# Causal attention: transposing the probabilities of query rows 4 to 7 by VectorE and transfers instead of TensorE

## What is computed

```python
qkv = jnp.einsum('bse,ehd->bshd', x, qkv_w) + qkv_b
q, k, v = jnp.split(qkv, 3, axis=-1)
logits = jnp.einsum('bqhd,bkhd->bhqk', q, k)
logits = logits / jnp.sqrt(jnp.asarray(q.shape[-1], logits.dtype))
mask = jnp.tril(jnp.ones((q.shape[1], q.shape[1]), dtype=jnp.bool_))
logits = jnp.where(mask, logits, _large_negative_number(logits.dtype))
probs = jax.nn.softmax(logits, axis=-1)
attn = jnp.einsum('bhqk,bkhd->bqhd', probs, v)
return jnp.einsum('bqhd,hde->bqe', attn, out_w) + out_b
```

## Time and profile before

| | before |
|---|---|
| runs | 1651.46, 1652.03, 1653.18 us |
| median | 1652.03 us |
| profiled execution: span | 1651.1 us |
| TensorE busy | 1635.6 us (99%), 9922 matmuls |
| VectorE busy | 1330.1 us (81%) |
| ScalarE busy | 1005.6 us (61%) |
| GpSimd busy | 888.1 us (54%) |
| granted TensorE clock, mean | 0.999 |

### The profile page before, as it was taken

How to read it: one execution, slowest core, us unless ns; L and a number is a source line. 1 busy time by engine, 2 the same in 40 slices (tenths; PEclk the granted TensorE clock), 3 DMA queues, 4 the chain that set the end, 5 groups by cost and what they waited for, 6 DMA issues and landing times.

```text
span 1651.1 us, 29212 instructions
## 1 busy us (share of the span) xinstructions
PE 1635.6 (99%) x9922; PEld 1044.6 (63%) x9922; DVE 1330.1 (81%) x2763; ACT 1005.6 (61%) x2025; POOL 888.1 (54%) x686
## 2 busy tenths in 40 slices
PE   8999999999999999999999999999999999999998
PEld 6765566556655665566556655665666766676767
DVE  7677777777777778777777777776999999999997
ACT  4466666666666666666666666666676557566562
POOL 4133333334333333433333433334999999999995
PEclk9999999999999999999999999999999999999999
DMA  8000000000000000000000000010000000000000
GB/s 182 27 1 1 2 1 1 1 2 1 1 1 1 1 1 1 1 1 2 1 1 1 1 2 1 1 27 1 1 1 7 7 1 8 7 2 7 1 7 13
DMA packets 30036, 13.55 MB, mean 8 GB/s; under 512 B 17066, under 2 KB 29380, under 8 KB 29892
## 3 DMA queue, kind: packets, MB, share of 16 engines
q1 hardware_dynamic: 29892, 11.70, 3.1%
HBM read 9.60 MB, written 2.10 MB: 7 GB/s over the span
## 4 chain that ended last, share of the span: by engine, by line
PE 96%; DVE 2%; ACT 1%; issue 1%; POOL 0%; DVEq 0%; POOLq 0%; ACTq 0%
PE pair L1007 17%; PE flip L1024 17%; PE accum L1045 11%; PE pair L2755 9%; PE misc L972 7%; PE flip L2778 5%; PE misc L1091 4%; PE flip L2767 4%; PE misc L985 3%; PE accum L1069 3%; PE flip L2815 3%; PE accum L2767 2%; PE accum L2778 2%; PE accum L1073 2%; PE flip L2801 1%; PE flip L949 1%
## 5 line engine op out<-in xcount | busy, mean ns | idle before, releaser
L391 POOL TENSOR_SCALAR probs<-probs,recip 128x256 f32<-128x256 f32 (+5 forms) x448 | 331.2, 754 | 688.2 <-DVE recip L647 688.0
L466 ACT ACTIVATE probs<-pair,neg_max 128x768 f32<-128x768 f32 (+5 forms) x448 | 332.0, 749 | 208.9 <-DVE neg_max L629 208.9
L629 DVE TENSOR_REDUCE neg_max<-pair 128x1 f32<-128x768 f32 (+7 forms) x512 | 372.3, 753 | 32.8 <-PE pair L1007 9.6
L1024 PEld LDWEIGHTS flip<-ident,probs 128*128 128x128 f32 x2048 | 228.0, 141 | 142.3 <-issue 65.4
L1007 PE MATMUL pair<-qk_sb 64*128 64x512 f32 (+3 forms) x1536 | 291.6, 505 | 0.8 <-ACT probs L466 0.7
L1024 PE MATMUL flip<-ident,probs 128*128 128x128 f32 x2048 | 280.0, 277 | 1.8 <-ACT slots L428 1.8
L428 ACT ACTIVATE slots<-flip 128x512 f32<-128x512 f32 x320 | 183.6, 595 | 155.7 <-PE flip L1024 155.7
L620 DVE TENSOR_TENSOR pair<-pair,mask 128x128 f32<-128x128 f32 x512 | 136.9, 292 | 79.4 <-PE pair L1007 79.4
L1045 PE MATMUL accum<-slots,v_sb 128*64 128x512 f32 (+3 forms) x1024 | 192.7, 519 | 0.0
L2755 PE MATMUL pair<-slow_sb,h_T 128*128 128x512 f32 x384 | 179.9, 594 | 1.2 <-ACT probs_last L466 1.0
L1587 POOL TENSOR_TENSOR prod<-xnT,qs 128x1024 f32<-128x1024 f32 (+3 forms) x32 | 180.2, 5639 | 0.9 <-DVE qs L2296 0.9
(11 more groups left out here) (230 smaller groups left out, 2542.0 us busy)
## 6 DMA issues: line engine op xcount, KB each, us to landing
out<-x SPq DMA_DIRECT2D x8, 256.0 KB, 2.3
x<-in_L_attn_x SPq DMA_DIRECT2D x3, 512.0 KB, 5.8
slow_sb<-in_L_attn_w_slow SPq DMA_DIRECT2D x3, 512.0 KB, 8.0
w_qk<-in_L_attn_qkv_w SPq DMA_DIRECT2D x2, 512.0 KB, 7.5
xn<-in_L_ffn_W SPq DMA_DIRECT2D x1, 1024.0 KB
x<-in_L_attn_x SPq DMA_DIRECT2D x2, 256.0 KB, 3.3
w_v<-in_L_attn_qkv_w SPq DMA_DIRECT2D x1, 512.0 KB, 8.1
bv_bc<-in_L_attn_qkv_b SPq DMA_DIRECT2D x1, 512.0 KB, 8.0
```

Of the source, the lines that this page charges most:

```text
L391: pool.tensor_scalar(part, part, recip[:, u % 2, row, h:h + 1], 0.0, ALU.mult, ALU.add).then_inc(scaled, 1)
L466: act.activation(dst, pair[h][:, lo:hi], ACT.Exp, bias=neg_max[:, u % 2, row, h:h + 1], accum_out=row_sum[:, u % 2, row, h:h + 1]).then_in ...
L629: dve.tensor_reduce(out=neg_max[:, u % 2, row, h:h + 1], in_=pair[h][:, lo:hi], axis=AX.X, op=ALU.max, negate=True).then_inc(max_ready, 1)
L1024: last = pe.transpose(flips[bank][:, P * k:P * (k + 1)], src[:, P * k:P * (k + 1)], ident[:])
```

## The change

The probabilities of query rows 4 to 7 are no longer transposed by TensorE. ScalarE writes them to a new buffer `big` with the 128 keys of each block cut into four groups of 32, so that for a key group `b` all its blocks of both heads lie together. GpSimd scales them there. VectorE transposes them in place, every 32x32 block for itself (`turn`, eight instructions a unit, one for each row and head). What is left is to exchange blocks between groups of 32 partitions: SyncE issues for each row sixteen SBUF-to-SBUF transfers (`move`), one from each of four source groups of partitions to each of four target groups, 32 partitions by 256 (r + 1) bytes, from `big` to `across`. That is 64 transfers a unit. `weigh_high` reads `across` in runs of 32 columns, in two groups: rows 6 and 7, then rows 4 and 5.

With it go these changes:
- Rows 0 to 3 are still flipped by TensorE, only their own 10 blocks a head (`flip`, names f0 to f3), kept by ScalarE alone in `low_T`; `weigh_low` reads them.
- Row 3 no longer uses `pair`. Its scores go to the two flip banks (`score_last`), so that `pair` holds four steps a unit.
- The three banks flip 0, flip 1 and `misc` are one pool (`BANK`, `take`).
- The mask is added once for a step, to all its rows and both heads (`cover`).
- The bias of the values is added to the attention (`keep_att`) instead of the values; ScalarE now keeps values, projections and the attention.
- Everything of a unit's transposing and weighing is done one unit later, and all orders are new.

The diff, cut to its core:

```diff
+HIGH_ROWS = (6, 7), (4, 5)
+DEEP = 8, 6
+LOW = 4
...
-LAST_BANK = 0
...
+BANK = {('f1',): 0, ('f0',): 2, ('f2', 1): 1, ('v', 1): 2, ('v', 0): 2, ('f3', 1): 0, ('f2', 0): 1, ('qk', 1, 0): 2, ('f3', 0): 0, ('qk', 1, 1): 2, ('qk', 0, 1): 2, ('o', 0): 0, ('qk', 0, 0): 2, ('o', 1): 1}
+MOVES = P // 32
...
+        big = sb("big", [P, MOVES * 64 * sum(r + 1 for g in HIGH_ROWS for r in g)])
+        across_flat = sb("across", [P, MOVES * 2 * 64 * sum(DEEP)])
+        low_T = sb("low_T", [P, 2, LOW, 512])
...
-        probs = sb("probs", [P, 2, 2, S])
...
-        slots = sb("slots", [P, (2 * ROWS + 1) * 512])
...
+        probs_low = e_buf[:].rearrange("p c n -> p (c n)"), qs[:].rearrange("p c n -> p (c n)")
...
+        def probs_of(row, h):
+
+            if row < LOW:
+                return probs_low[h][:, LOW_AT[row]:LOW_AT[row] + P * (row + 1)]
+            return row_probs[row][:, :, :, 32 * h:32 * (h + 1)]
...
+            def move(u, row):
+                if done(u):
+                    return
+                g = group_of(row)
+                sp.wait_ge(turned[row], 2 * (u + 1))
+                if u:
+                    sp.wait_ge(weighed, weighed_at(u - 1, "high", g))
+                else:
+                    sp.wait_ge(branch_ready, 2 * B)
+                i = HIGH_ROWS[g].index(row)
+                for a in range(MOVES):
+                    for b in range(MOVES):
+                        sp.dma_start(across[g][32 * b:32 * (b + 1), a, i, 0:row + 1, :], row_probs[row][32 * a:32 * (a + 1), b, :, :]
+                                     ).then_inc(moved[row], 16)
+
+            for u in range(UNITS):
+                move(u - 1, 6)
+                move(u - 1, 5)
+                move(u - 1, 4)
+                move(u, 7)
+            tails["sync"] = move
 
...
-                part = probs_last[:, h, :] if step_of(row) == LAST else probs[:, h, step_of(row) % 2, lo:hi]
+                part = probs_of(row, h)
...
+                if row >= LOW:
+                    if u:
+                        act.wait_ge(moved[row], 16 * MOVES * MOVES * u)
+                    dst = dst.rearrange("p b j k -> p j b k")
+                    src = src.rearrange("p (j b k) -> p j b k", b=MOVES, k=32)
...
+                wide = mask[:].unsqueeze(1)
+                if len(STEP_ROWS[step]) == 2:
+                    wide = wide.unsqueeze(1).broadcast_to([P, 2, 2, P])
+                else:
+                    wide = wide.broadcast_to([P, 2, P])
+                dve.tensor_tensor(part, part, wide, ALU.add).then_inc(covered, 1)
...
+            def turn(u, row, h):
...
+                part = probs_of(row, h)
+                dve.wait_ge(scaled, scaled_at(u, row, h))
+                dve.transpose(part, part).then_inc(turned[row], 1)
...
+            def score_last(u):
...
+                for h in range(2):
...
+                    part = slice(D * h, D * (h + 1))
+                    pe.matmul(flips[h], lhsT=q[part, P * r:P * (r + 1)], rhs=k[part, 0:512], start=True, stop=True
+                              ).then_inc(bank_made[h], 1)
...
+            def flip(u, name, *h):
...
+                k = take(u, name, *h)
+                row = int(name[1])
+                for n, each in enumerate(h if h else range(2)):
+                    pe.wait_ge(scaled, scaled_at(u, row, each))
+                    for c in range(row + 1):
+                        at = P * ((row + 1) * n + c)
+                        last = pe.transpose(pool_of[k][:, at:at + P], probs_of(row, each)[:, P * c:P * (c + 1)], ident[:])
+                last.then_inc(bank_made[k], 1)
...
-            def weigh_high(u, lo, hi):
...
+            def weigh_high(u, g, lo, hi):
...
+                    for row in HIGH_ROWS[g]:
+                        pe.wait_ge(moved[row], 16 * MOVES * MOVES * (u + 1))
...
+                for j in range(lo, hi):
+                    own = int(j == DEEP[g] - 1)
+                    for h in range(2):
+                        dst = accum[D * h:D * (h + 1), 0:2 * P].rearrange("p (a i q) -> p a i q", a=MOVES, i=2)[:, :, own:2, :]
+                        last = pe.matmul(dst, lhsT=values_of(u, j, h), rhs=across[g][:, :, own:2, j, 32 * h:32 * (h + 1)],
+                                         start=j == 0, stop=j == DEEP[g] - 1)
+                if hi == DEEP[g]:
+                    weighed_at.meet(u, "high", g)
+                    last.then_inc(weighed, 1)
...
+                for j in range(LOW):
...
+                        last = pe.matmul(accum[D * h:D * (h + 1), P * j:512], lhsT=values_of(u, j, h), rhs=low_T[:, h, j, P * j:512],
+                                         start=j == 0, stop=j == LOW - 1)
...
+            last_move = tails["sync"]
+            last_move(UNITS - 1, 6)
+            last_move(UNITS - 1, 5)
+            last_move(UNITS - 1, 4)
```

More of the change, by code:

```diff
@@ L109, in banks_of, with __init__ @@
     return [k for k in range(2) if lo < 512 * (k + 1) and hi > 512 * k]
-GROUPS = (1, 0)
-EARLY = (('qk', 0, 1), ('qk', 1, 0))
+GROUPS = (0, 1)
+EARLY = (('qk', 1, 0), ('qk', 1, 1))
 class Tally:
-    def __init__(self, order, last=()):
+    def __init__(self, order, last=(), tail=()):
         self.order, self.at, n = order, {}, 0
         for body in range(-1, UNITS + 1):
-            for key, ahead in order:
+            for key, ahead in [(key, -1) for key in tail] if tail and body == UNITS else order:
                 if 0 <= body + ahead < UNITS or (body + ahead == UNITS and key in last):
@@ L462, in softmax @@
-                if owner >= 0:
-                    for f in range(1 if before == LAST else 2):
-                        bank = FLIP_BANK[before, h, f]
-                        act.wait_ge(flipped[bank], flips_at[bank](owner, before, h, f))
-                act.activation(dst, pair[h][:, lo:hi], ACT.Exp, bias=neg_max[:, u % 2, row, h:h + 1],
-                               accum_out=row_sum[:, u % 2, row, h:h + 1]).then_inc(probs_ready, 1)
-            def keep_att(u, g):
+                if step_of(row) != LAST:
+                    exps_at.meet(u, row, h)
@@ L614, in cover @@
-            def cover(u, row, h):
-                if done(u):
-                    return
-                covers_at.meet(u, row, h)
-                lo, hi = place_of(row)
-                dve.wait_ge(scores_ready, scores_at(u, step_of(row), banks_of(row)[-1]))
-                dve.tensor_tensor(pair[h][:, hi - P:hi], pair[h][:, hi - P:hi], mask[:], ALU.add).then_inc(covered, 1)
+                covers_at.meet(u, step)
+                part = diagonals(step)
+                if step == LAST:
+                    for h in range(2):
+                        dve.wait_ge(bank_made[h], uses_at[h](u, "s4"))
+                else:
+                    dve.wait_ge(scores_ready, max(scores_at(u, step, k) for k in range(2)))
@@ L992, in score @@
                 scores_at.meet(u, step, bank)
-                if step == 0:
-                    pe.wait_ge(misc_kept, max(misc_at(u, "qk", c, half) for c in range(2) for half in range(2)))
-                before, owner = (step - 1, u) if step else (LAST, u - 1)
-                if before == LAST and bank != LAST_BANK:
-                    before = LAST - 1
+                projected(u)
+                before, owner = (step - 1, u) if step else (LAST - 1, u - 1)
                 if owner >= 0:
-                    pe.wait_ge(probs_ready, max(exps_at(owner, r, h) for r in STEP_ROWS[before] if bank in banks_of(r) for h in range(2)))
+                    for r in STEP_ROWS[before]:
+                        if bank in banks_of(r):
+                            for h in range(2):
+                                pe.wait_ge(*exponents_of(owner, r, h))
                 q, k = qk_sb[:, u % 2, 0, :], qk_sb[:, u % 2, 1, :]
@@ L1018, in flip, with free_accum @@
+            def free_accum(u, *part):
+                use = weighed_at(u, *part)
                 if use > 1:
-                    pe.wait_ge(flip_kept[bank], use - 1)
+                    pe.wait_ge(att_kept, use - 1)
                 else:
-                    pe.wait_ge(ffn_added, 2 * (B - 1))
-                src = probs_last[:, h, :] if step == LAST else probs[:, h, step % 2, 512 * f:512 * (f + 1)]
-                for k in range(GB):
-                    last = pe.transpose(flips[bank][:, P * k:P * (k + 1)], src[:, P * k:P * (k + 1)], ident[:])
@@ L1025, in flip, with has_values @@
-                last.then_inc(flipped[bank], 1)
-            def weigh_high(u, lo, hi):
+                    pe.wait_ge(ffn_added, 2 * B)
+            def has_values(u, f):
+                for i in range(2):
+                    k, use = use_of(u - u % 2 + f, "v", i)
+                    pe.wait_ge(bank_kept[k], use)
+            def weigh_high(u, g, lo, hi):
                 if done(u):
@@ L1052, in weigh_first, with weigh_low @@
+                if hi == DEEP[g]:
+                    weighed_at.meet(u, "high", g)
+                    last.then_inc(weighed, 1)
+            def weigh_low(u):
```

(3 more changed lines are left out.)

797 lines of the change are left out of this document (393 added, 404 removed).

## The result

The changed kernel takes 1968.19 us (median of 4 runs, 1965.68 to 1971.22) against 1652.59 us (1651.46 to 1653.18): **1.191 times as long, 95% interval 1.189 to 1.193**. The forecast was 1516, with a range from 1468 to 1600 and a chance of 0.08 for the mechanism that came.

A forecast was written before the change was run, and what follows sets the result against it. TensorE, full at 33.06 us a unit, was taken as the bound; afterwards the softmax loop at 28.4. Saving 149.1 over 32 units, less 1.7 and 11.7, turned a 1651.1 span into 1515.4; forecast 1516 us, range 1468 to 1600.

The forecast's parts named there:

- The SyncE queue: SyncE issuing 64 transfers a unit at 0.41 us each: 26.3 us, just under TensorE's 26.8; bounds 0.31 to 0.55.
- a step of the queue above 0.45: Sign, in SyncE's transfers of a row, that the forecast is wrong in size; starts 0.41 us apart were expected.
- slower by the same mechanism: Rival: at 0.51 us a transfer SyncE's queue cancels the whole gain; at 0.55 the time is 1732; chance 0.08.
- The end: After unit 31, next layer's first transposes wait for row 4's transfers: 25.9 us instead of 14.2, losing 11.7.
- VectorE: VectorE's load falls from 24.65 to 23.4 us a unit, with eight new block transposes costing 8.2.
- The rival that pays per block: VectorE's transposes pay 0.292 us for each 128-column block, 15.2 us a unit; time 1615 to 1665; chance 0.08.
- ScalarE, GpSimd: Loads a unit: ScalarE 20.1 us after copies go and come, GpSimd 12.1 us with its scaling unchanged.
- The ring: Four score steps a unit, each waiting for earlier exponentials to read its bank: 7.0, 6.9, 7.2, 7.3, sum 28.4 us.
- the steps of rows 6 and 0 and of rows 4 and 2: Two of the four score steps a unit, summed through masks, maxima and exponentials: 6.9 and 7.3 us.
- TensorE's floor: TensorE's own work a unit: 33.06 less 6.3 us for 52 transposes gone, 26.8 us.
- the weighing in runs of 32 columns: TensorE's matmuls over high rows reading columns in runs of 32 elements: priced at nothing extra; weighing 5.90 us before.
- the four projections: TensorE's projections in a unit, priced from start to start at 0.86 us each.

The follow-up runs named there:

- p1_prices: Kernel before the change, with eight series of added transfers (SBUF to SBUF, stores, loads) in the idle SyncE queue: 1651.76 us.
- e2_half_size: Changed kernel, each of the 64 transfers a unit carrying only half of its key blocks after unit 0: 1961.71 us.
- e3_half_count: Changed kernel, only eight of the sixteen transfers of each row made after unit 0, at full size: 1575.58 us.
- e6_twelve: e1_four with each transfer cut into three by key blocks, 48 transfers a unit with all the bytes: 1686.46 us.
- e1_four: Changed kernel with four transfers a row instead of sixteen, same bytes, keys reordered to 4k + b: 1554.04 us.
- e4_deviation: e1_four with GpSimd's variance work of a finished batch moved from ahead of row 1's scaling to the start of the following unit: 1529.47 us.
- e7_order: e4_deviation, row 3's head 1 flip between value projections, scores of rows 6 and 0 before projection, row 7's second exponential before value copy: 1551.61 us.

## Why the prediction was wrong, step by step

- **The SyncE queue: the step that failed.** "The stores are the only long series issued into an idle queue, so I take 0.41: 64 x 0.41 = 26.3 us a unit". It is 0.655 and 41.9. The bounds, 0.31 to 0.55, did not hold it either. The eight stores of the earlier trace rows are spread over 394 us and go to the output; they are not a series, and not this kind of transfer. The forecast named the sign, a step of the queue above 0.45. p1_prices shows the parts: 0.507 alone, 0.084 behind another, 0.043 of gap, and 0.02 on average for the few long ones of up to 1.9 us. e2_half_size shows that at these sizes bytes have no part in it, e3_half_count, e6_twelve and e1_four that the number does.
- **The direction.** The rival "slower by the same mechanism" had its place and break-even (0.51) right. With 0.655 in its sum: 1651.1 + 32 x (41.9 - 33.06) + 13 = 1947, 19 short of the span. The queue also starts only at 85.8, once unit 0 has its branches behind it; and the end is longer, next point.
- **The end.** Predicted: 25.9 us from unit 31 to the next layer's first flips. In e4_deviation, where the queue is out of the way, TensorE's timeline has the start of unit 1 and those flips at

```profile
94.65 2.75 PE L1063 MATMUL both<-qk_sb 64*128 64x512 f32 x8
...
1006.86 0.30 PE L2807 MATMUL flips_all<-ident,nrm 128*128 128x128 f32 x1 [2.68 <-ACT nrm L1884]
```

  and 1006.86 - 94.65 - 31 x 28.58 = 26.2. Not foreseen: the next layer takes 1529.1 - 1006.9 = 522.2 us from there, where before it took 1651.1 - 1134.16 = 516.9. The window over its first 50 us:

```profile
1007.00:1057.00 50.00, 49.66 (x193) 29.59 (x193) 41.70 (x80) 30.76 (x48) 35.43 (x13) 0.90 0.00 1
```

  TensorE is busy throughout, but at a granted clock of 0.90, so for a part of it at 1.2 and not 2.4 GHz; in the same 50 us of the kernel before (1134 to 1184) it is 1.00. In e4_deviation the clock was 0.56 over the first 5 of these 50 us and 0.50 over the next 5; in the 11 us ahead, TensorE had stood still for 2.07, 0.66 and 2.68 us at a clock of 1.00. A tenth of 50 us is 5 us.
- **VectorE.** In the changed kernel the block transposes of row 7 take 1233 ns (1.2 predicted) and those of row 4 814 (count | busy us, mean ns | idle before):

```profile
L711 DVE STREAM_TRANSPOSE big<-big 128x1024 f32<-128x1024 f32 x64 | 78.9, 1233 | 0.0
L711 DVE STREAM_TRANSPOSE big<-big 128x640 f32<-128x640 f32 x64 | 49.6, 814 | 2.6 <-POOL big L432 2.6
```

  The load is 23.71 us a unit (23.4 predicted). The rival that pays per block is out: a wide instruction costs 1.20 to 1.27 ns for each of its columns (1233 / 1024, 814 / 640), so 128 of them within it cost about 0.16 us. The Trainium skill ("VectorE: DVE Perf Modes", the three transpose paths) has 311 ns for one 128x128 transpose, in bf16. A wide fp32 one pays half of that for each 128 columns; a lone 128x128 no run here has, and the two rows extended down to 128 columns (1.09 ns a column and 0.12 us) would give it an estimated 0.26 us.
- **ScalarE, GpSimd.** 19.7 and 11.6 us a unit, 20.1 and 12.1 predicted.
- **The ring.** Hidden behind the queue in the changed kernel, it shows in e4_deviation: steps of 7.34, 6.80, 7.15 and 7.28 us, 28.6 in all, against 7.0, 6.9, 7.2 and 7.3, 28.4. The sizes held, in part by luck: I had summed the steps of rows 6 and 0 and of rows 4 and 2 through the softmax, and what fills them is TensorE's own work, which happens to be as long. I took TensorE's floor at 26.8; its own work is 28.6 - 0.7 = 27.9, and e7_order shows that it binds in the step of rows 6 and 0. The term that I had priced at nothing, the weighing in runs of 32 columns, does cost nothing: (635.12 - 632.60) + (659.24 - 655.85) = 5.91 us against 5.90 before. A good part of the missing 1.1 is in the four projections, priced at 0.86 from start to start. With transposes behind them that holds; with scores, weighing or a join behind them, as now, they take 0.96 to 1.18 (636.24 - 635.12 = 1.12), 4.4 us a unit against 3.65 in the kernel before.
- **A term that I left out.** The variance work on GpSimd, 24.6 us in all between e1_four and e4_deviation. The queue covered it in the changed kernel: there the row 7 transfers of all units are 41.2 to 43.0 us apart, with no long step at a new batch.
- **The sum without the queue.** e4_deviation's span is 1529.1 against 1515.4. Unit 1 starts at 94.7, not at 61.6 + 30.7 = 92.3, which makes 2.4; 31 units at 0.18 more make 5.6; the clock some 5.3; the end 0.3; 13.6 together.

So the direction and nearly all of the error come from the price of one transfer, which was multiplied by 2048. The other errors are what e1_four has above the forecast, 38 us: the variance work with 24.6 and the 13.6 of the last point.

## What to carry to other kernels

A queue that issues small transfers back to back is a resource like an engine: count its instructions, and price them from the same kind of transfer, in a row, not from solitary ones of another kind. The Trainium skill ("DMA: Bandwidth & Descriptors", section "Rules for kernel authors") advises to join many small transfers into a large one; here the trace agrees, and by choosing which key goes to which column, 64 transfers became 16 with the same bytes, and 1968 us became 1554 and, with one step moved, 1529. When a bound is lifted, read the work that was hidden under it again: here it was 4 us of GpSimd in three of 32 units.
